# A decoder layer on one core: own PSUM banks for the second batch's projections, three feed-forward tiles let in before the attention ends, and new orders for all five queues

## The reference

```
x = x + attn(layernorm(x))                      # 16 heads of 16, RoPE, causal softmax, Wqkv, Wo
x = x + xattn(layernorm(x), ctx, mask)          # one head over ctx, no projections
x = x + ffn(layernorm(x))                       # 8 experts of 176, top 2 by softmax gate, and a shared one of 352
ffn: y = sum_e comb[n, e] * ((silu(x w1_e) * (x w2_e)) w3_e) + (silu(x sw1) * (x sw2)) sw3
```

## The kernel before

| step | what it does | engines |
|---|---|---|
| `ln1`, `ln2`, `ln3` (`ln1n` ... on ACT) | moments on DVE, 1/sqrt on POOL, normalising on ACT | DVE, POOL, ACT |
| `xt`, `v`, `vm` | transpose of batch b's normalised rows; values and their two low parts | PE, ACT, DVE |
| `qk`, `sh` | queries and keys of one tile of 128 tokens (two for each batch), RoPE, split into high and low parts | PE, DVE, POOL, ACT |
| `tr` (`kt` on DVE) | transposes of queries and keys, four for each tile | PE, ACT, DVE |
| `m`, `mt` | 12 score products for each batch that give only the row maxima; their transpose, which SP then moves by DMA into `q_t` | PE, DVE, ACT, SP |
| `s`, `h`, `pv` | 12 score products for each batch with exp; every three are split into halves (`h`: high on ACT, low on POOL); the product with the values | PE, ACT, POOL, DVE |
| `on`, `ot`, `wo` | normalised attention output, its transpose, Wo and the residual | DVE, PE, ACT |
| `t2`, `xs`, `pt`, `ro` | cross attention of batch b | all but POOL |
| `t3`, `lg`, `rk`, `ct`, `cb` | third transpose, gate logits, rank, comb to HBM (SP) and back, spread over partitions (`cb.0` for batches 0 and 1, `cb.1` for 2 and 3) | all |
| `w12`, `w3` | split of the feed-forward weights into high and low halves, ACT then POOL, 14 steps each | ACT, POOL |
| `up.m`, `dn.m` | feed-forward tile m: 14 tiles of 128 hidden columns for each of two groups of 512 tokens. `up` is 12 products and silu, gate and comb; `dn` is 12 products into the output banks | PE, ACT, DVE |
| `early.n`, `late.n` | n products of a tile of zeros, that nothing reads | PE |
| `zero` | zeroes unused places of the second `q_t` buffer | DVE |

## Time and profile before

### The profile page before, as it was taken

One profiled execution on the slowest core, in us unless ns is written; L12 is line 12 of the kernel. 1 busy time (PEld: TensorE's weight loads), 2 busy tenths in 40 slices (PEclk: granted clock), 3 DMA queues, 4 the chain that ended last, 5 costly groups with the idle time before them and its releaser, 6 DMA issues.

```text
span 282.7 us, 4951 instructions
## 1 busy us (share of the span) xinstructions
PE 267.5 (95%) x1834; PEld 212.2 (75%) x1844; DVE 166.5 (59%) x361; ACT 172.6 (61%) x288; POOL 120.1 (42%) x133
## 2 busy tenths in 40 slices
PE   7879989989999999889899999999999999999994
PEld 2448746867777777666688878998899888888884
DVE  5567973754787667943454466836366625444563
ACT  8689328989893799878876664544635532232230
POOL 5399851794875619998665912001011000000000
PEclk9999999999999999999999999999999999999999
DMA  7990000000000207002004910000000169000002
GB/s 231 371 378 9 0 3 5 0 4 0 2 0 4 75 5 260 0 5 74 2 3 113 253 42 3 1 3 0 0 2 16 58 175 227 10 2 1 0 0 77
DMA packets 11879, 17.09 MB, mean 60 GB/s; under 512 B 1904, under 2 KB 8272, under 8 KB 11856
## 3 DMA queue, kind: packets, MB, share of 16 engines
q1 hardware_dynamic: 11856, 16.78, 19.8%
HBM read 15.63 MB, written 1.08 MB: 59 GB/s over the span
## 4 chain that ended last, share of the span: by engine, by line
PE 69%; ACT 9%; POOL 9%; DMA 5%; issue 3%; DVE 2%; SPq 1%; DVEq 0%; ACTq 0%; POOLq 0%
PE bank L758 28%; PE bank L866 14%; PE bank L771 8%; PE bank L812 3%; PE bank L765 3%; DMA gate_raw<-gate 3%; PE bank L798 2%; PE bank L919 2%; POOL prob_lo L392 2%; DMA q_t<-negm_t 2%; PE bank L836 2%; POOL w_lo L399 2%; PE bank L791 2%; PE bank L816 2%; ACT q_t L493 2%
## 5 line engine op out<-in xcount | busy, mean ns | idle before, releaser
L392 POOL TENSOR_TENSOR prob_lo<-prob,prob_hi 128x1536 f16<-128x1536 f32 x16 | 49.7, 3118 | 22.7 <-ACT prob_hi L512 22.6
L758 PE MATMUL bank<-x_hi,w_hi 128*128 128x512 f32 x112 | 45.5, 407 | 0.3 <-ACT prob L505 0.3
L758 PE MATMUL bank<-x_hi,w_lo 128*128 128x512 f32 x112 | 44.2, 395 | 0.0
L758 PE MATMUL bank<-x_lo,w_hi 128*128 128x512 f32 x112 | 44.0, 393 | 0.0
L549 ACT CAST h_hi<-h_c 128x512 fp32r<-128x512 f32 x28 | 17.3, 620 | 41.8 <-DVE h_c L735 23.2
L726 DVE TENSOR_TENSOR h_c<-bank,h_s 128x512 f32<-128x512 f32 x28 | 19.3, 690 | 31.2 <-PE bank L758 21.6
L583 DVE TENSOR_REDUCE negm<-bank 128x2 f32<-128x512 f32 (+1 forms) x48 | 31.2, 684 | 6.8 <-PE bank L793 3.9
L866 PE MATMUL bank<-w_hi,h_hi 128*128 128x256 f32 x112 | 32.5, 290 | 0.1
L740 DVE TENSOR_TENSOR h_lo<-h_c,h_hi 128x512 fp32r<-128x512 f32 x28 | 20.2, 728 | 19.5 <-ACT h_hi L549 19.5
L866 PE MATMUL bank<-w_lo,h_hi 128*128 128x256 f32 x112 | 31.7, 283 | 0.0
L866 PE MATMUL bank<-w_hi,h_lo 128*128 128x256 f32 x112 | 31.6, 283 | 0.0
(11 more groups left out here) (127 smaller groups left out, 587.3 us busy)
## 6 DMA issues: line engine op xcount, KB each, us to landing
w_raw<-w SPq DMA_DIRECT2D x3, 1792.0 KB, 8.6
comb_b<-comb_dram SPq DMA_DIRECT2D x8, 256.0 KB, 5.2
res<-x SPq DMA_DIRECT2D x4, 256.0 KB, 6.9
ctxt_s<-ctx_t SPq DMA_DIRECT2D x4, 256.0 KB, 5.6
ctx_s<-ctx SPq DMA_DIRECT2D x4, 256.0 KB, 5.6
out<-res SPq DMA_DIRECT2D x8, 128.0 KB, 1.8
comb_b<-comb_dram SPq DMA_DIRECT2D x4, 224.0 KB, 5.2
wqkv_s<-wqkv SPq DMA_DIRECT2D x1, 768.0 KB, 5.3
```

Source lines behind the costliest of these rows:

```text
L392: eng.tensor_tensor(prob_lo[:, b % 2], prob[:, b % 2], prob_hi[:, b % 2], ALU.subtract)\
L758: ins = pe.matmul(dst, a(k), c(k), start=(k == 0 and i == 0), stop=(k == kt - 1 and i == 2))
```

## The change

1. `xt.1` and `v.1` use bank 7 in place of bank 0, and `qk.1` uses bank 5 in place of bank 1. `xt.1` then waits for no reader and `qk.1` for no RoPE; in exchange the first score step `m.0` waits for two RoPEs, and the first `pv` for `vm.1`.
2. Feed-forward tiles 0, 1 and 2 all use banks 3 and 4, so `up.0` needs the last `mt` but no longer the last exp; that wait moves to `up.3`. Each of the three waits until the gate product of the one before has read the pair. From tile 3 on, pairs alternate (banks 5 and 6, then 3 and 4). `silu` of tile 0 and the first `w3` copies wait for the scores of the third batch, the `w3` copies from the seventh on for all scores; to that end `w3_hi` moves behind the `h` buffers. `cb.0` no longer waits for the last `pv`.
3. The hidden columns are renumbered, the shared expert's first (the same tiles came first before), and the `w12` pieces in the order in which they are used.
4. All five orders are new. Of the 52 products of zeros within PE's list 14 stay: `early` from 33 to 11, `late` from 19 to 3. No other step is added or taken away.

```
-        h1_bank, h2_bank = [bank[3], bank[4]], [bank[5], bank[6]]
+        h1_bank, h2_bank = [bank[3], bank[5]], [bank[4], bank[6]]
+
+        def h_pair(m):
+            return 0 if m < EARLY else (m - EARLY + 1) % 2
+
+        def h_last(m):
+            return max([q for q in range(m) if h_pair(q) == h_pair(m)], default=-1)
+
+        def x1_bank(b):
+            return ps_out if b == 1 else ps_x1
+
+        def qk_bank(n):
+            return ps_s[0] if n == 1 else ps_qk
...
 PE "xt":
-                    if b:
-                        pe.wait_ge(s["v_mid"], 2 * b)
+                    if b >= 2:
+                        pe.wait_ge(s["v_mid"], 4 * b - 6)
...
 PE "up":
                     if m == 0:
                         pe.wait_ge(s["mt_ok"], B)
+                        pe.wait_ge(s["xn_lo_ok2"], GT // S)
+                    if m == EARLY:
                         pe.wait_ge(s["p_exp"], 3 * NG * B)
-                        pe.wait_ge(s["xn_lo_ok2"], GT // S)
...
 ACT "w3":
                     if b == 0:
                         act.wait_ge(s["w3_in"], 16)
+                        act.wait_ge(s["s_ps"], 3 * NG * (B - 1))
+                    if b == 6:
                         act.wait_ge(s["s_ps"], 3 * NG * B)
-                        act.wait_ge(s["o_ps"], NG * B)
```

Of the orders, the parts that matter below. PE's start, before and after:

```
-        xt.0 qk.0 v.0 qk.1 early.10 xt.1 tr.0 tr.1 qk.2 tr.2 tr.3 v.1 tr.4 tr.5 m.0 m.1 tr.6 m.2 tr.7 m.3 qk.3
-        m.4 m.5 xt.2 m.6 m.7 v.2 m.8 m.9 qk.4 m.10 m.11 early.3 qk.5 mt.0 tr.8 tr.9 early.3 tr.10 s.0 s.1 tr.11
+        xt.0 qk.0 qk.1 v.0 xt.1 qk.2 tr.0 tr.1 v.1 tr.2 tr.3 qk.3 tr.4 m.0 tr.5 m.1 tr.6 m.2 tr.7 m.3 xt.2
+        early.1 m.4 m.5 m.6 m.7 m.8 m.9 m.10 m.11 early.3 mt.0 tr.8 tr.9 v.2 tr.10 s.0 tr.11 s.1 tr.12 s.2 tr.13
```

PE around the last batch's scores, before and after:

```
-        s.39 s.40 pv.11 s.41 s.42 late.1 s.43 late.6 s.44 s.45 late.1 s.46 late.2 t3.1 late.3 pv.12 lg.1 s.47
-        pv.13 late.1 up.0 ct.1 pv.14 ot.2 up.1 wo.2 pv.15 up.2 dn.0 dn.1 t2.2 up.3 xs.2 up.4 pt.2 up.5 ro.2 dn.2
+        m.45 pt.1 m.46 m.47 ro.1 mt.3 pv.9 s.36 s.37 pv.10 s.38 late.1 t3.1 s.39 s.40 pv.11 lg.1 s.41 up.0 s.42
+        s.43 ct.1 late.1 up.1 ot.2 pv.12 wo.2 s.44 pv.13 s.45 s.46 dn.0 s.47 up.2 t2.2 up.3 pv.14 xs.2 up.4 pt.2
```

ACT in the same stretch after, and POOL's start before and after:

```
+        h.10 w12.8 s.33 xs.1 w3.0 pt.1 w3.1 s.34 w3.2 s.35 w3.3 mt.3 h.11 w3.4 vm.3 s.36 ln3n.1 s.37 s.38 t3.1 s.39
+        s.40 h.12 lg.1 s.41 up.0 h.13 ct.1 dn.0 up.1 ot.2 s.42 s.43 s.44 w12.9 dn.1 s.45 s.46 h.14 ln2n.2 s.47 up.2
...
-        ln1.0 ln1.1 tr.7 qk.0 ln1.2 sh.0 qk.1 ln1.3 w12.0 sh.1 w12.1 w12.2 w12.3 w12.4 w12.5 w12.6 qk.2 sh.2 qk.3
+        ln1.0 ln1.1 qk.0 sh.0 qk.1 qk.2 sh.1 w12.0 ln1.2 ln1.3 qk.3 w12.1 sh.2 tr.7 sh.3 h.0 qk.4 h.1 sh.4 h.2 h.3
```

More of the change, by code:

```diff
@@ L30 @@
 FE = E * I // P
+SH = FT - FE
+EARLY = 3
 GT = 512
@@ L51 @@
     "SP": """
-        ln1.0 mt.0 mt.1 mt.2 ro.0 w3.0 ct.0 mt.3 ro.1 ct.1 cb.0 ct.2 y.0 ct.3 cb.1 y.1
+        ln1.0 mt.0 mt.1 mt.2 ct.0 ro.0 w3.0 mt.3 ct.1 cb.0 ro.1 y.0 ct.2 ct.3 cb.1 y.1
     """,
     "POOL": """
-        ln1.0 ln1.1 tr.7 qk.0 ln1.2 sh.0 qk.1 ln1.3 w12.0 sh.1 w12.1 w12.2 w12.3 w12.4 w12.5 w12.6 qk.2 sh.2 qk.3
-        sh.3 qk.4 qk.5 h.0 h.1 sh.4 sh.5 h.2 h.3 h.4 h.5 ln2.0 h.6 h.7 qk.6 sh.6 ln3.0 qk.7 sh.7 h.8 h.9 w12.7 w12.8
-        w12.9 ln2.1 h.10 w12.10 w12.11 w12.12 h.11 w12.13 h.12 ln3.1 h.13 h.14 h.15 w3.0 w3.1 ln2.2 w3.2 w3.3 w3.4
@@ L58 @@
-        w3.5 w3.6 w3.7 w3.8 w3.9 w3.10 w3.11 w3.12 w3.13 ln3.2 ln2.3 ln3.3
+        ln1.0 ln1.1 qk.0 sh.0 qk.1 qk.2 sh.1 w12.0 ln1.2 ln1.3 qk.3 w12.1 sh.2 tr.7 sh.3 h.0 qk.4 h.1 sh.4 h.2 h.3
+        qk.5 sh.5 w12.2 ln2.0 w12.3 h.4 h.5 qk.6 sh.6 ln3.0 h.6 qk.7 h.7 sh.7 w12.4 w12.5 h.8 ln2.1 w12.6 h.9 h.10
+        w3.0 w3.1 w12.7 ln3.1 h.11 w12.8 w3.2 h.12 h.13 w3.3 w12.9 ln2.2 h.14 w3.4 w3.5 w3.6 h.15 w12.10 w3.7 ln3.2
+        w12.11 w3.8 w3.9 w3.10 ln2.3 w3.11 w12.12 w3.12 w3.13 w12.13 ln3.3
@@ L59 @@
     """,
     "ACT": """
[L61 to L70, removed]
@@ L71 @@
-        dn.16 up.17 dn.17 up.18 dn.18 up.19 dn.19 up.20 dn.20 up.21 dn.21 up.22 dn.22 up.23 dn.23 up.24 dn.24 up.25
-        dn.25 up.26 up.27 dn.26 dn.27
+        ln1n.0 xt.0 ln1n.1 w12.0 sh.0 xt.1 w12.1 v.0 vm.0 tr.0 tr.1 sh.1 v.1 w12.2 tr.4 tr.5 ln1n.2 w12.3 w12.4 sh.2
+        vm.1 w12.5 sh.3 mt.0 xt.2 tr.8 tr.9 s.0 s.1 tr.12 s.2 h.0 tr.13 s.3 s.4 s.5 h.1 s.6 s.7 sh.4 s.8 s.9 h.2
+        s.10 s.11 h.3 ln1n.3 mt.1 tr.16 tr.17 s.12 s.13 sh.5 v.2 ot.0 s.14 vm.2 tr.20 s.15 tr.21 s.16 s.17 ln2n.0
@@ new lines @@
+        xt.3 t2.0 h.4 w12.6 h.5 xs.0 s.18 s.19 pt.0 s.20 sh.6 s.21 h.6 s.22 ln3n.0 s.23 mt.2 t3.0 tr.24 h.7 lg.0
+        sh.7 s.24 s.25 tr.25 s.26 h.8 ct.0 tr.28 ot.1 s.27 tr.29 s.28 v.3 s.29 s.30 h.9 s.31 ln2n.1 w12.7 t2.1 s.32
+        h.10 w12.8 s.33 xs.1 w3.0 pt.1 w3.1 s.34 w3.2 s.35 w3.3 mt.3 h.11 w3.4 vm.3 s.36 ln3n.1 s.37 s.38 t3.1 s.39
+        s.40 h.12 lg.1 s.41 up.0 h.13 ct.1 dn.0 up.1 ot.2 s.42 s.43 s.44 w12.9 dn.1 s.45 s.46 h.14 ln2n.2 s.47 up.2
+        t2.2 up.3 w3.5 w3.6 w3.7 h.15 xs.2 dn.2 pt.2 dn.3 w12.10 up.4 w12.11 up.5 ln3n.2 dn.4 t3.2 dn.5 up.6 lg.2
@@ L73 @@
+        w12.12 w3.8 w3.9 w3.10 up.7 ct.2 dn.6 up.8 w3.11 ot.3 dn.7 w12.13 ln2n.3 up.9 t2.3 dn.8 up.10 w3.12 xs.3
+        dn.9 pt.3 dn.10 w3.13 up.11 ln3n.3 up.12 dn.11 t3.3 up.13 dn.12 dn.13 lg.3 up.14 dn.14 up.15 up.16 dn.15
+        ct.3 dn.16 up.17 dn.17 up.18 dn.18 up.19 dn.19 up.20 dn.20 up.21 dn.21 up.22 up.23 dn.22 up.24 dn.23 up.25
+        dn.24 up.26 dn.25 up.27 dn.26 dn.27
     """,
     "DVE": """
-        ln1.0 zero.0 ln1.1 zero.1 qk.0 ln1.2 v.0 qk.1 vm.0 ln1.3 qk.2 kt.2 kt.3 v.1 m.0 m.1 kt.6 m.2 m.3 kt.7 vm.1
@@ L81 @@
[L81 to L84, removed]
+        ln1.0 ln1.1 qk.0 ln1.2 qk.1 ln1.3 v.0 qk.2 vm.0 kt.2 kt.3 v.1 qk.3 m.0 m.1 kt.6 m.2 kt.7 m.3 m.4 m.5 m.6 m.7
@@ new lines @@
+        m.8 m.9 m.10 m.11 zero.0 zero.1 kt.10 kt.11 vm.1 qk.4 kt.14 kt.15 m.12 m.13 pv.0 m.14 m.15 m.16 m.17 m.18
+        m.19 m.20 m.21 m.22 m.23 pv.1 pv.2 qk.5 pv.3 on.0 kt.18 v.2 kt.19 vm.2 wo.0 ln2.0 kt.22 kt.23 m.24 m.25 m.26
+        m.27 xs.0 m.28 m.29 xc.0 m.30 qk.6 m.31 m.32 ro.0 ln3.0 pv.4 m.33 m.34 m.35 qk.7 t3.0 pv.5 lg.0 kt.26 pv.6
+        rk.0 pv.7 on.1 kt.27 kt.30 wo.1 kt.31 ln2.1 m.36 m.37 m.38 m.39 m.40 m.41 m.42 v.3 xs.1 m.43 m.44 m.45 pv.8
+        xc.1 m.46 m.47 ro.1 ln3.1 pv.9 vm.3 pv.10 t3.1 pv.11 lg.1 rk.1 up.0 on.2 pv.12 dn.0 up.1 wo.2 ln2.2 dn.1
@@ new lines @@
+        qk.4 s.3 s.4 tr.14 early.3 tr.15 s.5 s.6 m.12 m.13 pv.0 s.7 m.14 m.15 s.8 m.16 s.9 m.17 s.10 m.18 m.19
+        s.11 m.20 m.21 pv.1 m.22 m.23 qk.5 mt.1 pv.2 tr.16 tr.17 early.2 pv.3 s.12 s.13 tr.18 tr.19 s.14 s.15
+        early.2 ot.0 tr.20 wo.0 tr.21 s.16 tr.22 xt.3 s.17 tr.23 s.18 s.19 m.24 m.25 t2.0 m.26 m.27 xs.0 m.28
+        m.29 qk.6 m.30 pt.0 m.31 s.20 m.32 ro.0 s.21 m.33 s.22 pv.4 m.34 qk.7 m.35 s.23 pv.5 mt.2 t3.0 tr.24
+        tr.25 lg.0 tr.26 pv.6 s.24 s.25 v.3 s.26 pv.7 s.27 ct.0 tr.27 tr.28 s.28 late.1 ot.1 tr.29 tr.30 wo.1
@@ L229, in up_weights @@
         def up_weights(i):
-            piece = (i + UPW - 2) % UPW
+            piece = i % UPW
             parts = ((w1_raw, w1_hi, w1_lo), (w2_raw, w2_hi, w2_lo))[i // UPW]
@@ L866, in down @@
                         ins = pe.matmul(y_tile(t), a[:, m % 2, tok], c[:, j, :],
-                                        start=(n == 0 and i == 0 and t % 2 == 0), stop=(n == FT - 1 and i == 2),
+                                        start=(j == 0 and i == 0 and t % 2 == 0), stop=(j == FT - 1 and i == 2),
                                         skip_group_check=True)
-                    if n == FT - 1 and t == 1:
+                    if j == FT - 1 and t == 1:
                         ins.then_inc(s["y_ps"], 1)
@@ L1022, in up @@
     def up(w, shared):
-        return np.concatenate([w.reshape(E * I, C), shared, np.zeros((hidden - E * I - IS, C), w.dtype)]).T
+        return np.concatenate([shared, np.zeros((hidden - E * I - IS, C), w.dtype), w.reshape(E * I, C)]).T
     w3 = a["L0_ffn_w3"]
-    down = np.concatenate([w3.transpose(0, 2, 1).reshape(E * I, C), a["L0_ffn_sw3"].T,
-                           np.zeros((hidden - E * I - IS, C), w3.dtype)])
+    down = np.concatenate([a["L0_ffn_sw3"].T, np.zeros((hidden - E * I - IS, C), w3.dtype),
+                           w3.transpose(0, 2, 1).reshape(E * I, C)])
     inv = (1.0 / np.float32(10000.0) ** (2.0 * np.arange(DH // 2, dtype=np.float32) / DH)).astype(np.float32)
```

101 lines of the change are left out of this document (48 added, 53 removed).

## The result

The changed kernel takes 272.16 us (median of 4 executions, 270.96 to 273.15), the kernel before 284.17 us beside it: 0.957 of it, with a 95% interval of 0.951 to 0.962. That is 12.0 us less, where 13.2 us had been forecast.

The account below looks back on a forecast made before the run. PE bounds the feed-forward part; 33 us lay open before it. Windows 37.5 + 20.5 + 30 + 26 + 22.3, then 127.3 + 3 + 3.8, gave 270.4 us span, taken as 269.4; with 1.6 us beyond span, 271.0 us, range 264.5 to 279.5.

Parts of the forecast that it names:

- the start: Stretch from 0 to `s.0`: three parts bring `s.0` from 43.7 to 37 to 37.5 us, 6.5 us gained.
- first batch: Window from `s.0` to `s.12`: bound by `s.12` behind the fourth `h` on POOL, 20.5 us against 21.1.
- second batch: Window from `s.12` to `s.24`: 30 us against 30.2, nothing gained but 2 us more work done.
- third batch: Window from `s.24` to `s.36`: chain through POOL relieved and ACT lighter, 26 us against 28.7, 2.7 us gained.
- fourth batch: Window from `s.36` to `s.47`: feed-forward tiles come in, ACT at 93%, 22.3 us against 15.8, for 7.8 us of content.
- the rest: After `s.47`: 127.3 us of work left instead of 137.3, with 3 us of waits against 2.1.
- the own bank: Second part of the start: `xt.1` no longer waits for bank 0, beginning at about 14.3 us instead of 17.97.
- The first part: In the start: POOL's RoPE sum no longer stands behind the gate and mask work, 2 us sooner.
- The third: In the start: `qk.4`, `qk.5`, two RoPEs and nearly all POOL `w12` behind `mt.0`; `mt.0` at about 33 us.
- These three go behind it: Third batch: three weight pieces on POOL, 3.72 us, move from ahead of `ln2.1` to behind it.
- The table loads: ACT, fourth batch: two more loads at 1.28 us each, following the rows; the skill's page would add about 2.7 us.
- The clock as a rival: Attention part: with 38 of 52 zeros gone the clock might fall to 1.2 GHz; 25 us there gives 292 us; chance 0.05.

Follow-up runs that it names:

- before_gate_late: Kernel before with one step moved, POOL's split of the gate weights and mask to behind `sh.3`: 284.21 us (ratio 0.999).
- after_no_early_filled: Changed kernel with no feed-forward tile ahead of the last exp and products of zeros in the holes this leaves: 279.98 us (ratio 0.981).
- before_no_zeros: Kernel before without any of the 52 products of zeros in PE's list: 289.54 us (ratio 1.017).

## Why the prediction was right, and where not

The time lay 1.2 us above the forecast, in the range, and the two terms that carried the forecast, the start and the work that is gone from behind `s.47`, are the two that carry the result.

| step | forecast | measured |
|---|---|---|
| `mt.0` / `s.0` | 33 / 37.5 | 34.4 / 38.3 |
| `s.12` (first batch 20.5) | 58 | 60.4 (22.2) |
| `s.24` (second batch 30) | 88 | 91.3 (30.9) |
| `s.36` (third batch 26) | 114 | 118.7 (27.4) |
| `up.0` | before 123 | 124.9 |
| `s.47` (fourth batch 22.3) | 136.3 | 138.4 (19.6) |
| the rest (127.3 + 3) | 130.3 | 128.2 |

*The start.* The size was nearly right (5.5 for 6.5). Of its three parts the own bank is the one shown: 5.0 us with what it lets the orders do. The first part, POOL's RoPE "2 us sooner", is worth nothing alone (before_gate_late). The third, the RoPEs and products moved behind `mt.0`, was not tried alone.

*First and second batch.* I had POOL as full as ACT, 21.7 us from the first `h` to the fifth, and took 20.5; the window took 22.2, a term too small by 1.7 us. The order was right, for the fourth `h` ends at 59.74 and `s.12` starts at 60.45. The fill was not: POOL was busy for 15.12 of the 22.20 us, its first `h` began at 43.62, and the fifth at 74.34. The second batch came 0.9 us over.

*Third batch.* This step failed as an argument: "These three go behind it", 2.7 us gained. The window shrank by 1.3 us, and the very move, made alone on the kernel before, cost 1.7 us. What pulled the second batch's tail ahead (`t2.1` from 118.9 to 106.3, while `s.36` moved by 5) I did not isolate. In PE's new list `t2.1`, `xs.1`, `pt.1` and `ro.1` stand among the maxima and no longer behind them, and on ACT five `w12` pieces of 0.6 us left this stretch, with five `w3` pieces of 0.4 us in their place. The chain that ended last, which went through ACT and POOL for most of this window before, goes through PE from 91.3 to 115.3 us now, and then through the DMA of the maxima.

*Fourth batch and the rest.* Content moved ahead of `s.47`, as forecast, but the price was mis-sized, and not ACT set it. I had ACT at 20.7 us, 7.0 more than before, with a fill of 93%. It was busy for 16.20 us, 2.5 more than before, and the two loads, 2.57 us, are in that figure: 83% of the window. PE was busy for 19.51 of the 19.60 us and the chain runs through it. By my count of PE's content, 17.6 us, 2.0 us of the window stood open where 6.0 had before (9.8 of 15.8): the tiles went into PE's holes. That the window is PE's is read from the chain; no run relieved ACT alone. The rest lost 0.9 us to waits where I had 3. And I missed the wait for the last exp, which `up.2` covers. For after_no_early_filled that made my expectation 2 us too low at its upper end.

That the sum met the span within 0.1 us (270.4 forecast, 270.3 measured) is luck: `s.36` came 4.7 us late, the fourth batch was 2.7 us and the rest 2.1 us shorter than forecast. The 1.2 us that the forecast lay too low are the 1.0 that I took off that sum and 0.2 more from span to time.

*The table loads.* They take 1.28 us each, with the next activation at once behind where its input is there. The 2.66 us of the Trainium skill (ScalarE: Activation LUTs, What ACT_TABLE_LOAD costs) are not seen in any of the rows.

*The clock as a rival.* It did not happen in the changed kernel's median, so 1.00 was the right reading. But the reason was half right. I argued from one sparse stretch that the zeros were not needed; in the kernel before they were (5.2 us). That they can go in the changed one because real work has taken their places is my reading; no run shows it apart. Without the bank or without the tiles the clock took 2.4 and 2.9 us on top. The price was too high as well: I took 0.85 us lost for each us at 1.2 GHz, and these two kernels spent 10.2 and 13.6 us there, 0.2 us lost for each, so the 292 us of this rival was far too much.

## What to carry to other kernels

When PE is full from some point on, count what content lies ahead of that point: a tile let in early is worth its own length and the wait that it covers, less what it adds to the stretch that it is let into. That is little where PE has holes, even if another engine looks fuller. A step on the chain that ended last may be filling a wait that is there anyway: look at what its engine would wait for next before you move it. When an edit opens a hole in TensorE's work, fill the hole with idle products once, so that the edit's own price and the clock's are told apart.

## What I had not expected of the hardware

A small hole can cost more than its own length. An edit that left PE busy for 1.56 of 3.50 us was followed by 3.3 us at 1.2 GHz, and in the kernel without zeros one fall lasted 13.5 us; why that one lasted I did not try. It is not settled by the hole alone: in the changed kernel's trace PE is busy for 0.57 of the 3.40 us from 115.7 on, at the same place, and the clock stayed at 1.00. Two of its four executions had a mean clock of 1.00 and two 0.994; with 11 products of zeros there none of six was under 0.997. The kernel before does it too: of 19 executions beside before_no_zeros, fifteen with a mean clock of 0.998 or more took 283.9 to 284.7 us, and four with 0.993 or 0.994 took 285.1 to 286.3.
